# Row maxima of an attention group found and sent in two halves of 512 query rows

## The reference

```python
    qkv = jnp.einsum('bsi,oi->bso', x, w_qkv) + b_qkv
    ...
    attn = jnp.einsum('bhqd,bhkd->bhqk', q, k) * scale
    attn = jax.nn.softmax(attn, axis=-1)
    vals = jnp.einsum('bhqk,bhkd->bhqd', attn, v)
```

## Time and profile before

| | us |
|---|---|
| median of 3 runs | 1705.62 (1703.88 to 1716.97) |
| the profiled execution | 1706.73 |
| its span, first to last instruction | 1704.6 |
| DVE busy | 1147.9 (67%) |
| PE busy | 1402.5 (82%) |
| ACT busy | 749.3 (44%) |
| mean granted TensorE clock | 0.895 |

### The profile page before, as it was taken

How to read it: one execution, slowest core, us unless ns; L and a number is a source line. 1 busy time by engine, 2 the same in 40 slices (tenths; PEclk the granted TensorE clock), 3 DMA queues, 4 the chain that set the end, 5 groups by cost and what they waited for, 6 DMA issues and landing times.

```text
span 1704.6 us, 30558 instructions
## 1 busy us (share of the span) xinstructions
PE 1402.5 (82%) x8111; PEld 670.2 (39%) x8112; DVE 1147.9 (67%) x2760; ACT 749.3 (44%) x1155; POOL 587.2 (34%) x749
## 2 busy tenths in 40 slices
PE   7978799968969969869689598778999999999800
PEld 4541223312313313213133122545777776777600
DVE  7868699867949949768679462433555555555579
ACT  4650477645736636547457376001333333333200
POOL 3000100451453345334514545250445544544400
PEclk9995799988969979979889799889999999999955
DMA  6889523343433333443333345654554544555397
GB/s 222 271 258 147 165 45 85 79 121 92 89 98 97 80 102 98 109 118 81 120 88 100 98 115 164 196 176 125 149 150 152 159 150 145 153 152 152 118 379 316
DMA packets 222780, 243.50 MB, mean 143 GB/s; under 512 B 96925, under 2 KB 188445, under 8 KB 222562
## 3 DMA queue, kind: packets, MB, share of 16 engines
q1 hardware_dynamic: 195394, 170.02, 36.8%
q0 software_dynamic: 20096, 62.83, 10.0%
q10 hardware_dynamic: 7200, 9.51, 1.6%
HBM read 133.98 MB, written 108.28 MB: 142 GB/s over the span
## 4 chain that ended last, share of the span: by engine, by line
PE 62%; DVE 15%; another core or an unknown queue 8%; issue 5%; ACT 1%; DMA 1%; POOL 0%; DVEq 0%; SPq 0%; POOLq 0%; ACTq 0%
PE psO L1130 12%; PE psE L1117 11%; PE ex_psGU L1575 11%; PE psM L1107 9%; DVE piece_max L1010 8%; PE ex_psY L1590 6%; PE ex_psX L1566 4%; PE psM L503 2%; PE psGU L1427 2%; DVE wide L1713 2%; PE ex_psA L1584 2%; PE psX L1438 1%; DVE wide L1715 1%; PE psM L522 1%
## 5 line engine op out<-in xcount | busy, mean ns | idle before, releaser
L1010 DVE TENSOR_REDUCE piece_max<-psM 128x1 f32<-128x512 f32 x1024 | 644.8, 682 | 187.3 <-remote 98.2
L1072 ACT ACTIVATE wide<-psE 128x1024 f32<-128x1024 f32 x512 | 499.3, 1021 | 363.1 <-PE psE L1117 254.7
L1107 PE MATMUL psM<-wide 48*128 48x512 bf16 x1024 | 345.7, 413 | 130.5 <-DVE piece_max L1010 104.6
L1117 PE MATMUL psE<-wide 49*128 49x512 bf16 (+1 forms) x2048 | 344.9, 393 | 0.7
L1659 POOL DMA_INDIRECT results<-vals_inv,ex_pair x223 | 214.5, 962 | 241.3 <-DVE vals_inv L1643 155.7
L1130 PE MATMUL psO<-wide 128*32 128x512 f32 x2048 | 285.0, 630 | 0.6 <-ACT wide L1072 0.6
L1107 PEld LDWEIGHTS psM<-wide 48*128 48x128 bf16 x1024 | 81.0, 95 | 492.1 <-DVE piece_max L1010 383.2
L1575 PE MATMUL ex_psGU<-wide,ex_xT 128*128 x892 | 238.6, 391 | 15.1 <-ACT ex_xT L1608 13.4
L1188 POOL DMA_INDIRECT lists<-rows,slot x168 | 163.0, 970 | 51.0 <-issue 47.6
L1575 PEld LDWEIGHTS ex_psGU<-wide,ex_xT 128*128 128x128 f32 x892 | 153.9, 192 | 40.3 <-issue 28.3
L1608 ACT ACTIVATE ex_xT<-ex_psX 128x256 f32<-128x256 f32 x223 | 85.6, 384 | 185.5 <-PE ex_psX L1566 141.0
(11 more groups left out here) (232 smaller groups left out, 1218.5 us busy)
## 6 DMA issues: line engine op xcount, KB each, us to landing
wide<-qk_parts SPq DMA_DIRECT2D x384, 64.0 KB, 3.0
wide<-results SPq DMA_DIRECT2D x16, 1536.0 KB, 9.9
rows<-lists SPq DMA_DIRECT2D x112, 160.0 KB
last_rows<-lists SPq DMA_DIRECT2D x111, 160.0 KB
qk_parts<-parts SPq DMA_DIRECT2D x32, 384.0 KB, 3.3
xin<-in_x_dram SPq DMA_DIRECT2D x16, 512.0 KB, 4.3
v_values<-vst SPq DMA_DIRECT2D x32, 256.0 KB, 3.7
wide<-v_values SPq DMA_DIRECT2D x16, 512.0 KB, 4.6
```

The lines of the kernel that those rows point to most:

```text
L1010: v.tensor_reduce(piece_max[:, (x * PAIRS + h) * KT + qt, kh:kh + 1], bank_of("piece", PIECES * group + n), AX.X, ALU.max, negate=True).th ...
L1072: nc.scalar.activation(probs[:, step % 2, 2 * pair:2 * pair + 2], psE[:, pair], ACT.Exp, scale=HD ** -0.5).then_inc(exp_ok, 1)
L1107: nc.tensor.matmul(bank_of(*user), qa[g][rows, h, qt * P:(qt + 1) * P], ka[g][rows, h, kh * 512:(kh + 1) * 512], start=True, stop=True).th ...
L1117: mm = nc.tensor.matmul(psE[:, pair, x], k[g][part, pair, kt * P:(kt + 1) * P], q[g][part, pair, qh * 512:(qh + 1) * 512], start=(q is qa) ...
```

## The change

The maxima of a group are found and sent in two halves, `k = 2 x group + qh`. `piece_at` now takes all heads of query half 0 first, then those of half 1. `finish(k)` joins and transposes 16 of the 32 columns. SP's `put_max(k)` is split into `store_max` and `load_max`; a load fills half of the row of `qa`. PE waits for rows at steps 0 and 8. `pieces_for` lets a group's pieces begin 11 steps ahead of it: half 0 in steps 5 to 12 of the group before (as its second 32 pieces were), half 1 in steps 13 to 15 and its own steps 0 to 4.

At the start PE issues 32 + 12 pieces of group 0 and goes to step 0. SP loads group 1, sends half 0, loads group 2, sends half 1, loads group 3, then constants and x. The wait for the constants on DVE moves to step 32. The 33 spare stores move into the loop, behind the rows of group 1's half 0. In later groups half 1's stores stand in `finish_values` in front of the inverse sums' store and its row loads behind it.

```diff
+            return divmod(4 * (step + AHEAD + KT), PIECES)
-            ahead, share = divmod(step + AHEAD, STEPS)
-            return ahead + 1, 4 * share
...
+            def store_max(k):
+                at = COLS * (k % QH)
+                sp.wait_ge(max_ready, k + 1)
                 for n in range(P // 32):
+                    sp.dma_start(env.max_d[at:at + COLS, n], neg_max_t[32 * n + at:32 * n + at + COLS, :]
+                                 ).then_inc(max_stored, 16)
+            def load_max(k):
+                group, qh = divmod(k, QH)
+                g, each = group % NG, COLS // 2
+                sp.wait_ge(max_stored, 4 * 16 * (k + 1))
...
-            for g in range(1, NG):
-                load_group(sp, env, 0, g)
+            load_group(sp, env, 0, 1)
             put_max(0)
+            load_group(sp, env, 0, 2)
+            put_max(1)
+            load_group(sp, env, 0, 3)
...
+                if group + 1 < NGR:
+                    store_max(2 * group + 3)
                 store_inverse(group)
+                if group + 1 < NGR:
+                    load_max(2 * group + 3)
...
-                    put_max(group + 1)
+                    put_max(2 * (group + 1))
+                if group == 0:
+                    store_spare()
...
-            for n in range(PIECES):
+            for n in range(HALF_PIECES):
                 piece_maximum(0, n)
+            dve.wait_ge(env.zeroed, 1)
             finish(0)
...
-            dve.wait_ge(env.zeroed, 5)
-            dve.wait_ge(const_in, 16 * 6)
+            dve.wait_ge(env.zeroed, 6)
...
-                if group < NGR and first + 4 == PIECES:
-                    finish(group)
+                if group < NGR and (first + 4) % HALF_PIECES == 0:
+                    finish(QH * group + first // HALF_PIECES)
...
-            for n in range(PIECES):
+            for n in range(HALF_PIECES + 4 * AHEAD):
                 piece(0, n)
-            pe.wait_ge(loaded[1], 16 * LOADS)
-            for n in range(4 * AHEAD):
-                piece(1, n)
...
-                if s == 0:
-                    pe.wait_ge(max_there, 2 * 16 * (group + 1))
+                if s % KT == 0:
+                    pe.wait_ge(max_there, 2 * 16 * (step // KT + 1))
```

More of the change, by code:

```diff
@@ L732, in attention_phase @@
     PIECES = HG * (S // P) * 2
+    HALF_PIECES = PIECES // QH
+    COLS = HG * KT // QH
     PAIRS = HG // 2
@@ L768, in piece_at @@
             n, kh = divmod(n, 2)
-            h, qt = divmod(n, KT)
-            return x, h, qt, kh
+            n, qt = divmod(n, KT // QH)
+            qh, h = divmod(n, PAIRS)
+            return x, h, qh, qt, kh
         def chunk_at(step):
@@ L783, in pieces_for, with put_max @@
         def pieces_for(step):
[L785 to L786 removed]
+            return divmod(4 * (step + AHEAD + KT), PIECES)
         @block.sync
         def _(sp):
[L790 to L792 removed]
+            def store_max(k):
+                at = COLS * (k % QH)
+                sp.wait_ge(max_ready, k + 1)
                 for n in range(P // 32):
[L795 to L796 removed]
+                    sp.dma_start(env.max_d[at:at + COLS, n], neg_max_t[32 * n + at:32 * n + at + COLS, :]
[4 more added lines that the diff above has]
+                sp.wait_ge(max_stored, 4 * 16 * (k + 1))
                 for x in range(2):
                     at = HALF * x + QROWS
[L799 to L801 removed]
+                    sp.dma_start(qa[g][at:at + 1, :, qh * S // QH:(qh + 1) * S // QH],
+                                 env.max_d[qh * COLS + x * each:qh * COLS + (x + 1) * each]
+                                 .rearrange("(h q) n r -> h (q n r)", h=PAIRS).unsqueeze(0)).then_inc(max_there, 16)
+            def put_max(k):
+                store_max(k)
+                load_max(k)
             def store(group):
@@ L848, in _ @@
             load_x(0)
[L849 to L853, removed]
             def finish_values(group):
@@ L865, in finish_values, with store_spare @@
                     load_values(c, env.inv, env.inv_d)
+            def store_spare():
+                sp.wait_ge(pads_built, 3)
+                spare = env.lists[E * CAP:LIST_ROWS].rearrange("(k p) n -> p k n", p=P)
+                for k in range(E):
+                    sp.dma_start(spare[:, k, 0:TARGET], env.pad_row[:, 0:TARGET]).then_inc(spare_in, 16)
+                sp.dma_start(spare[:, :, TARGET:ROW], spare_to[:].bitcast(F32)).then_inc(spare_in, 16)
             for group in range(NGR):
@@ L1008, in piece_maximum, with finish @@
                 dve.wait_ge(piece_done, PIECES * group + n + 1)
-                x, h, qt, kh = piece_at(n)
-                v.tensor_reduce(piece_max[:, (x * PAIRS + h) * KT + qt, kh:kh + 1], bank_of("piece", PIECES * group + n),
+                x, h, qh, qt, kh = piece_at(n)
+                v.tensor_reduce(piece_max[:, qh, (x * PAIRS + h) * KT // QH + qt, kh:kh + 1], bank_of("piece", PIECES * group + n),
                                 AX.X, ALU.max, negate=True).then_inc(piece_read, 1)
[L1013 to L1016, removed]
+            def finish(k):
+                part = piece_max[:, k % QH]
+                cols = slice(COLS * (k % QH), COLS * (k % QH + 1))
+                dve.wait_ge(piece_read, HALF_PIECES * (k + 1))
+                chain.link(v.tensor_tensor(neg_max[:, cols], part[:, :, 0], part[:, :, 1], ALU.min))
+                wait(dve, max_stored, 4 * 16 * k)
                 v.transpose(neg_max_t[:], neg_max[:]).then_inc(max_ready, 1)
```

9 lines of the change are left out of this document (6 added, 3 removed).

## The result

The changed kernel takes 1717.44 us (median of 20 runs, 1710.41 to 1724.75), the kernel before 1706.53 beside it: the ratio is 1.006, 95% interval 1.0044 to 1.0075. The profiled execution took 1717.72 us, 11.0 more than that of before. The forecast was 1699 with a range to 1714, so both the time and its sign were missed, by a change that does start the attention 33 us earlier. The prediction called anything within 1% the same, with a chance of 0.77: that came true, but not by its sum, which is off by 18 us.

What follows compares the result with a forecast made beforehand. DVE was taken as the bound, its maxima the largest group (644.8 us). Of 33.8 us gained at the start 18.3 remain; 18.3 - 3 - 4.9 - 3.1 = 7.3 us off 1706.73 gives 1699, range 1684 to 1714.

Steps and rivals of the forecast that it cites:

- (a): Start: DVE finds 32 maxima instead of 64 first and goes on at 147.0 instead of 180.82, 33.8 us earlier.
- (b): Group 0, half 1: maxima found at 169.4, rows issued by 173.3, needed near 175.5; no wait.
- (c): Rows of group 1's half 0, queued behind loads, constants and x, come late at step 16: a 4 us wait.
- (d): Spare stores on SP delay group 0's sums; DVE's reciprocal stands 10.7 us, leaving 18.3 of the 33.8 us.
- (e): Clock: slower steps after the two new stops, 2.1 us for the long and about 0.9 for the short, -3.
- (f): Second finish of each group on DVE: 14 more at 0.35 us, nothing hiding them, -4.9 us.
- (g): Last group: pieces run up to step 244, not 236, so 8 steps take 2.49 instead of 2.10 us, -3.1.
- (h): Eighth step of each group: new wait for half 1's rows, taken as 0, at most 0.5 us in each of 14.
- The stops "as they are": Stops beside POOL's scatters at the start of even groups from the fourth on: kept as unchanged by the change.
- Rival 2: DVE's wait for group 0's den does not happen or is far shorter: 1686, or 1681 us; chance 0.15.
- rival 3: Half 1's rows come late at step 8, behind the inverse: 14 x 1.7 = 24 us, 1723 us; chance 0.10 over 1706.
- rival 4: Scatter stops grow as POOL's scatters start nearer the projection: 2 us in each of six even groups, 1711 us; chance 0.13.

Runs made afterwards that it cites:

- e_consts: Changed kernel with the six constants and first chunk of x loaded behind group 1's first half of maxima: 1500.40 us, ratio 1.0032 to the kernel before.
- e_spare: Changed kernel with its 33 spare stores issued in two lots in front of group 2's and 3's maxima: 1500.90 us, ratio 1.0042 to the kernel before.

## Why the prediction was wrong, by its steps

- (a), (b): right. 33.1 against 33.8 us, no wait inside group 0 (0.2; 1.4 in kind 2).
- (c), (d), (e): right in mechanism and size. Rows of group 1 late by the constants and x (e_consts), the sums behind the spare stores (e_spare); the reciprocal at 226.75 against 225, idle 9.32 against 10.7. Together 18.8 against 18.5 us (the 15.5 by which 18.3 falls short of 33.8, and 3 for the clock). What the prediction saw rightly, that (c) lies inside (d), e_consts shows: 5.6 us gained and given back.
- **(f) failed.** "14 more, at 0.35" took the row of one finish, which stood at step 12, for all. That holds to 0.15 us in ten groups (0.43 in even ones, 0.5 in 3, 7 and 11). In three, 5, 9 and 13, the new finish meets POOL's addition and costs 4.6 us with the clock (3.6 in kind 2). 18.3 against 4.9: 13.4 us (the fourteenth, in group 15, shows nothing). The trace of the kernel before could have shown it. These are the additions of groups 3 and 5, which start at 314.9 and 432.8:

```profile
326.10 2.36 POOL L915 TENSOR_TENSOR xin<-xin,bo_g 128x1024 f32<-128x1024 f32 x1
...
445.98 2.36 POOL L915 TENSOR_TENSOR xin<-xin,bo_g 128x1024 f32<-128x1024 f32 x1
```

The new finish comes some 13.3 us into its group, at 328.2 and 446.1: the first addition has all but ended by then (328.46), the second has just begun.
- (g): right. 1.8 in group 15 and 1.5 in the last three steps of group 14 (7.6 us together, not 6.15), 3.3 against 3.1.
- (h): right in kind 1 (0). In kind 2, even groups lose up to 1.2 us there, 1.8 in all.
- The stops "as they are": they moved, in kind 1. The last steps of the odd groups to 13 take 30 us together instead of 20; steps 0 to 4 of groups 4, 6, ... 14 take 204 instead of 208, and their steps 9 to 14 117 instead of 124. In sum the rows "scatters" and "steps 9 to 14" fell, from 517 and 515 us to 513 and 514. The two kernels with added waits, whose attention is that of before, had 522 in the same rows, so a sum 2 us lower is within what one and the same attention code varies by; each of the three shifts is in both pairs. That they come from when POOL's scatters meet the steps is likely, but no run shows it.
- The experts were left out as unchanged code, without a reason given: +8.7 us in kind 1, as large as the whole forecast, and -7.5 in kind 2.

13.4 + 8.7, less some 1.4 of the rest, are the 20.7 us between -7.3 and the +13.4 of the two pairs of profiles (the medians differ by 10.9). Rival 2 did not happen, rival 3 did not in kind 1. Rival 3 was also mis-summed: by the slack of 0.8 us given in it, 2 us more cost a group 1.2 us and not 1.7, and the time would be 1716. Of rival 4, the last steps of the odd groups did grow, but the scatters and the steps around them not in sum. The slower side had its chance, but by another mechanism.

## What to carry to other kernels

Before a short two-input instruction is added or moved on VectorE, look in the trace at what GpSimd does at that very time, in every round and not in one: a 0.2 us instruction took 2.2 where they met, and cost 3.6 to 4.6 with the clock. When something is moved off a start, ask what stands in the same queue behind its new place, and repair the waits together, since each hides the next. A difference of some us in a phase of unchanged code is not noise before a second profile says so: a loop further down changed its price here with the length of the program in front of it.

## What the hardware showed beyond that

The kernel before took 1495 us (medians 1495.2 to 1495.4) in three sets and 1706 to 1708 in two others and the first. Group 4 of it in kind 1 and in kind 2 (the columns as above):

```profile
362.70:432.80 70.10, 52.12 (x340) 16.32 (x337) 43.51 (x74) 32.45 (x35) 26.17 (x41) 0.81 0.42 113
```

```profile
361.10:405.50 44.40, 44.31 (x339) 14.87 (x336) 43.15 (x74) 31.99 (x34) 26.15 (x40) 1.00 0.63 178
```

POOL is busy for the same 26.2 us, and 25.7 us of stop come or don't. The mean tile of the experts is 1.94 against 1.78 us. What sets the kind was not found; it is not the chip's number alone, and it holds for all runs of a set. A saving measured in one kind need not be one in the other, as the experts show: 8.7 us longer in one kind, 7.5 shorter in the other.

A turn of a loop that runs on five engines costs 0.95 or 0.68 us over a tile (2.58 and 2.31 against 1.63). The Trainium skill, Advanced Engine Details and Errata, section Control Flow Timing, gives about 108 ns for a compare-and-branch; the turn measured here is six to nine times that, and changes with the instructions in front of VectorE's loop.
